# FFN of a routed expert layer turned round: weights stationary, 320 token lanes per expert moving, rows scattered to expert regions instead of gathered by tile

## The reference

```python
x = x + attention(layernorm(x), ctx_1024, ctx_1024, Wq, bq, Wk, bk, Wv, bv)
xt = layernorm(x)                                  # 1024 tokens x 128
scores = xt @ gate_w.T                             # 8 experts
top_vals, top_idx = top_k(scores, 2); top_w = softmax(top_vals)
h  = silu(xt @ w1[e].T) * (xt @ w3[e].T)           # hidden 512, for each expert e
ye = h @ w2[e].T
x  = x + sum over the two chosen experts of top_w * ye
```

## Time and profile before

| | us |
|---|---|
| median of the runs | 136.7 |
| span of the profiled execution | 132.1 |
| PE busy in it | 102.9 |
| POOL busy | 84.8 |
| DVE busy | 78.5 |
| ACT busy | 44.1 |
| span from the first up product (L974) to the last w2 product (L1007) | 46.9 to 120.7 |

### The profile page before, as it was taken

The page is one execution under the profiler, slowest core; times in us unless marked ns, Lnnn a source line. Parts: engine busy times, 40 slices in busy tenths (PEclk is TensorE's granted clock), DMA queues, the critical chain, the costliest instruction groups (busy, mean ns, idle before and its releaser), DMA issues. The chain is left out here.

```text
span 132.1 us, 2609 instructions
## 1 busy us (share of the span) xinstructions
PE 102.9 (78%) x571; PEld 71.5 (54%) x571; DVE 78.5 (59%) x276; ACT 44.1 (33%) x109; POOL 84.8 (64%) x122
## 2 busy tenths in 40 slices
PE   6869976789899279998977897997897979993000
PEld 2245962525355057886866675765675756762000
DVE  0862589897897969996745554563465545632000
ACT  4035877647700013343242033333234033331000
POOL 3387008383975926498769968969979697573630
PEclk9999999869599955999999999999999999999855
DMA  3969999500130002032232322202222323222220
GB/s 108 264 250 424 424 429 404 171 6 0 48 113 18 23 9 39 0 45 24 36 45 40 40 32 27 40 20 40 40 40 40 36 24 40 36 24 20 20 20 0
DMA packets 8119, 11.42 MB, mean 86 GB/s; under 512 B 880, under 2 KB 6896, under 8 KB 7344
## 3 DMA queue, kind: packets, MB, share of 16 engines
q1 hardware_dynamic: 4592, 8.70, 17.7%
q0 software_dynamic: 3520, 2.64, 15.6%
HBM read 8.91 MB, written 2.43 MB: 86 GB/s over the span
## 5 line engine op out<-in xcount | busy, mean ns | idle before, releaser
L381 POOL DMA_INDIRECT out_rows<-y_sb,aid x20 | 31.9, 1595 | 13.9 <-SPq L290 6.4
L523 ACT ACTIVATE hidT<-bank 128x256 f32<-128x256 f32 x40 | 13.5, 382 | 45.6 <-PE bank L997 37.6
L1007 PEld LDWEIGHTS bank<-w_sb,hidT 128*128 128x128 f32 x160 | 19.6, 191 | 7.6 <-issue 7.0
L1007 PE MATMUL bank<-w_sb,hidT 128*128 x160 | 22.4, 283 | 1.6 <-ACT hidT L523 0.9
L360 POOL DMA_INDIRECT xg<-tok_rows,gid x18 | 18.4, 1020 | 7.5 <-DVE slot_w L764 3.4
L974 PE MATMUL bank<-w_hi,xgT 128*128 x40 | 20.1, 503 | 3.0 <-DVE xgT L756 3.0
L910 PE MATMUL bank<-ones 128*128 128x512 bf16 x66 | 20.5, 463 | 1.1 <-DVE ones L544 1.1
L516 ACT ACTIVATE sil<-bank 128x512 f32<-128x512 f32 x20 | 12.1, 603 | 13.9 <-PE bank L976 12.1
L773 DVE TENSOR_TENSOR hid<-bank,sil 128x512 f32<-128x512 f32 x20 | 13.8, 690 | 4.6 <-PE bank L976 2.6
L975 PE MATMUL bank<-w_lo,xgT 128*128 x40 | 16.5, 413 | 0.0
L976 PE MATMUL bank<-w_hi,xgT 128*128 x40 | 16.5, 412 | 0.0
(11 more groups left out here) (120 smaller groups left out, 144.3 us busy)
## 6 DMA issues: line engine op xcount, KB each, us to landing
w_sb<-in_w1T SPq DMA_DIRECT2D x2, 1024.0 KB, 9.9
w_sb<-in_w3T SPq DMA_DIRECT2D x2, 1024.0 KB, 13.6
w_sb<-in_w2T SPq DMA_DIRECT2D x2, 1024.0 KB, 17.2
tok_rows<-tok SPq DMA_DIRECT2D x1, 520.0 KB, 4.4
x_sb<-in_x SPq DMA_DIRECT2D x2, 256.0 KB, 3.2
out_rows<-x SPq DMA_DIRECT2D x2, 256.0 KB, 4.7
ctxT_sb<-in_ctxT SPq DMA_DIRECT2D x1, 480.0 KB, 5.1
out_rows<-y_sb,aid POOLq DMA_INDIRECT x20
```

What stands on the lines that cost most here:

```text
L381: nc.gpsimd.indirect_dma_start(out[:, :], bass.IndirectOffsetOnAxis(ap=aid[p][:, 0:1], axis=0), y_sb[p][:, :], None, compute_op=ALU.add).t ...
L523: nc.scalar.activation(hidT[p][:, h * H // 2:(h + 1) * H // 2], ps_hT[h][:, 0:H // 2], ACT.Copy).then_inc(s_hidT, 1)
L1007: last = mm(ps_y[:, 0:D], hidT[p][:, c * P:(c + 1) * P], w2_sb[:, bass.ds(e * H + c * D, D)], start=(c == 0), stop=(c == HC - 1))
```

## The change

The FFN is written anew, and with it what feeds it.

- Routing: each expert owns `REG` rows of a DRAM table `expert_rows`, the first `CAP` = 320 of them for its normal lanes. `count_before` adds the start of the region (one more small matmul with `region`), so that DVE gets the row of each choice with one product and one reduction (`slots`). One-hot products, tiles, `gather_id`, `add_id` and expert words are gone.
- SP first fills the normal lanes of all regions with empty rows (16 DMAs of 520-byte rows, 1.33 MB, between w3 and w2 in its queue). Then POOL writes each token's row to the regions of both its experts: 16 indirect DMAs of 128 rows, `s_put`. When all have landed, SP reads the regions back (two DMAs for each expert).
- FFN: eight experts, each with 320 moving lanes. PE transposes three blocks of rows, runs four times (w1 chunk, w3 chunk) and four w2 products, all plain 32-bit with 128 x 128 weights stationary, and transposes the result back in three blocks. ACT does SiLU and the copies, DVE the product and the weighing, POOL three indirect adds for each expert, after the adds of the expert before have landed.
- Tokens past 320 of one expert would go through a loop of overflow steps; DVE works out its tables (`overflow_table`, 17 more linked instructions) ahead of the FFN. With the counts above the loop runs zero times.
- No high and low parts of weights or tokens. ACT copies the normalised rows once more (`twin_rows`). The normalisation of group 1 is moved ahead of `top_two(0)`.

```diff
+CAP = 320
+LANES = [min(P, CAP - at) for at in range(0, CAP, P)]
+KT = len(LANES)
@@ sync @@
+            weights(w1_sb, w1T, s_w1)
+            weights(w3_sb, w3T, s_w3)
+            sp.wait_ge(s_empty, 2)
+            for e in range(E):
+                for rows, lanes, k in pieces(e):
+                    sp.dma_start(rows, empty_rows[0:lanes, k, :]).then_inc(s_filled, 16)
+            weights(w2_sb, w2T, s_w2)
...
-            sp.dma_start(rows, tok[:, :, :]).then_inc(s_rows, 16)
+            for t in range(B):
+                sp.wait_ge(s_put[t], 16 * K2)
+            for e in range(E):
+                for rows, lanes, k in pieces(e):
+                    sp.dma_start(xg[0:lanes, e, k, :], rows).then_inc(s_xg[e], 16)
@@ gpsimd @@
+            pool.wait_ge(s_filled, 32 * E)
+            for g in range(G):
+                pool.wait_ge(s_slot, g + 1)
+                pool.wait_ge(s_pw, 3 * (g + 1))
+                pool.wait_ge(s_twin, g + 1)
+                for t in range(g * TG, (g + 1) * TG):
+                    for c in range(K2):
+                        nc.gpsimd.indirect_dma_start(
+                            expert_rows[:, :], bass.IndirectOffsetOnAxis(ap=slot[:, c, t:t + 1], axis=0),
+                            tok[:, c, t, :], None).then_inc(s_put[t], 16)
...
+            for e in range(E):
+                if e:
+                    pool.wait_ge(s_add, 16 * KT * e)
+                if e == OV_AT:
+                    overflow()
+                for k in range(KT):
+                    pool.wait_ge(s_ysb, KT * e + k + 1)
+                    m = LANES[k]
+                    nc.gpsimd.indirect_dma_start(
+                        out[:, :], bass.IndirectOffsetOnAxis(ap=xg[0:m, e, k, D:D + 1].bitcast(U32), axis=0),
+                        y_sb[e % 2][0:m, k, :], None, compute_op=ALU.add).then_inc(s_add, 16)
@@ scalar @@
-            high_parts(0, 6)
             copy_x2nT(0)
-            high_parts(6, 11)
+            twin_rows(0)
             copy_x2nT(1)
...
@@ vector @@
-            normalise(1, 0, x1, x2n, s_x2n)
+            normalise(1, 0, x1, tok[:, 0], s_x2n)
             norm_stats(1, 1, x1)
+            normalise(1, 1, x1, tok[:, 0], s_x2n)
             dve.wait_ge(s_const, 11)
             top_two(0)
-            normalise(1, 1, x1, x2n, s_x2n)
+            pair_weights(0)
+            slots(0)
             top_two(1)
...
+            def hidden(j):
+                dve.wait_ge(s_sil, j + 1)
+                dve.wait_ge(s_b, j + 1)
+                if j >= HC:
+                    dve.wait_ge(s_d, j - HC + 1)
+                dve_.tensor_tensor(hT[j % HC][:, :], ps_b[j % 2][:, 0:CAP], sil[j % 2][:, :],
+                                   ALU.mult).then_inc(s_hid, 1)
+            def weigh(e):
+                dve.wait_ge(s_yr, e + 1)
+                if e > 1:
+                    dve.wait_ge(s_add, 16 * KT * (e - 1))
+                for k, m in enumerate(LANES):
+                    dve_.tensor_scalar(y_sb[e % 2][0:m, k, :], ps_yr[0:m, k * D:(k + 1) * D],
+                                       xg[0:m, e, k, D + 1:D + 2], None, ALU.mult).then_inc(s_ysb, 1)
@@ tensor @@
+            for t in range(B):
+                pe.wait_ge(s_put[t], 16 * K2)
+                keep_busy(ps_av, 5)
...
+            turn_rows(0)
+            for j in range(E * HC):
+                e, c = j // HC, j % HC
+                if j == HC * (OV_AT + 1):
+                    overflow()
+                up(j)
+                if j > 1:
+                    down(j - 2)
+                if c == 2 and e + 1 < E:
+                    turn_rows(e + 1)
+                if c == 3 and e:
+                    turn_out(e - 1)
+            down(E * HC - 2)
+            down(E * HC - 1)
+            turn_out(E - 1)
```

More of the change, by code:

```diff
@@ L163, in build @@
[L163 to L167, removed]
+        slot = sb("slot", [P, K2, B], U32)
+        count = sb("count", [P, E])
+        ov_over = sb("ov_over", [P, E, OVT])
+        ov_n = sb("ov_n", [P, E])
+        ov_end = sb("ov_end", [P, E])
+        ov_total = sb("ov_total", [P, 1], I32)
@@ new lines, in overflow @@
+            def overflow():
+                with pool.Fori(0, n) as i:
+                    pool.wait_ge(s_ovy, i + 1)
+                    pool.sem_inc(s_ovgo, 1)
+                    nc.gpsimd.indirect_dma_start(
+                        out[:, :], bass.IndirectOffsetOnAxis(ap=ov_id[:, 0:1], axis=0), ov_y, None,
+                        compute_op=ALU.add).then_inc(s_ovadd, 16)
+                    pool.wait_ge(s_ovadd, 16 * i + 16)
+                    pool.sem_inc(s_ovid, 1)
+            n = overflow_steps(pool)
@@ L530, in _, with overflow @@
[L530 to L538 removed]
+            n = overflow_steps(act)
+            def overflow():
+                with act.Fori(0, n) as i:
+                    act.wait_ge(s_ovt, i + 1)
+                    nc.scalar.activation(ov_xT, ps_ovxT, ACT.Copy).then_inc(s_ovxT, 1)
+                    act.wait_ge(s_ova, i + 1)
+                    nc.scalar.activation(ov_sil, ps_ova, ACT.Silu).then_inc(s_ovsil, 1)
@@ new lines, in copy_yT @@
+            def copy_yT(e):
+                act.wait_ge(s_d, HC * (e + 1))
+                if e > 1:
+                    act.wait_ge(s_yr, e - 1)
+                nc.scalar.activation(yT[e % 2][:, :], ps_y[e % 2][:, 0:CAP], ACT.Copy).then_inc(s_yT, 1)
+            copy_xgT(0)
+            for e in range(E):
+                if e == OV_AT + 1:
+                    overflow()
+                for c in range(HC):
+                    silu(HC * e + c)
+                    if c == 1 and e:
+                        copy_yT(e - 1)
+                    if c == 2 and e + 1 < E:
+                        copy_xgT(e + 1)
@@ L816, in _ @@
+            overflow_table()
+            for e in range(E):
+                if e == OV_AT + 1:
+                    overflow()
+                for c in range(HC):
+                    hidden(HC * e + c)
+                if e:
+                    weigh(e - 1)
+            weigh(E - 1)
         @block.tensor
@@ L913, in _ @@
             pe.wait_ge(s_ones, 1)
-            keep_busy(ps_rank[1], 14)
+            for i in range(8):
+                keep_busy(bank[i], 2)
             pe.wait_ge(s_const, 3)
```

736 lines of the change are left out of this document (250 added, 486 removed).

## The result

| | before | after |
|---|---|---|
| median of the runs, us | 136.5 (4 runs, 135.67 to 137.67) | 142.91 (4 runs, 140.83 to 143.42) |
| ratio, 95% interval | | 1.045 (1.032 to 1.059) |
| span of the profiled execution, us | 132.1 | 141.3 |
| that execution's own time, us | not known | 143.06 |
| PE busy, us | 102.9 | 104.9 |

What follows compares the result with a forecast made beforehand. PE's pace bounds the loop, POOL close behind. Front + 9.7, loop - 14.5, slow start - 1.1, tail + 6.3 sum to + 0.4 on the 132.1 span; with 4.6 outside it 137.1 us, range 129.5 to 146.

Steps and rivals of the forecast that it cites:

- The overflow loop: Loop of overflow steps in the FFN: taken to run zero times, given no term in the sum and no rival.
- PE's pace: FFN loop: 0.54 us a product, 0.59 for the transposes in and out, 7.05 us an expert, 56.4 for eight.
- The clock: Start of the FFN: PE's clock falls to half after a 2.9 us pause, 2.3 us lost, bounds 0 and 2.8.
- The front: Up to the first up product: first scatter at 30.0, 1.32 us a step, first up product at 56.6, 9.7 later.
- The fills: Front: filling the regions with empty rows ends at 26 expected, 30 at full price, hardly in the way.
- The tail: After the last w2 product: adds wait for landings, 7.1 us a group; 17.7 us instead of 11.4, + 6.3.
- The median above the span: Outside the span: 4.6 us added to the 132.5 span, as the median before stood that far above its span.
- Scatter at the price of an add: Slower rival, front: a scatter costs what an add does, 8.7 us later, 146.2; chance 0.3 together with the DVE stop.
- POOL stopped by DVE: Slower rival, front: DVE's work holds up POOL's scatters, ending 7.2 us later, 144.3; chance 0.3 together with the dearer scatter.
- No gaps and a full clock: Faster rival: scatters and adds without 0.30 us gaps, clock holds at the FFN's start, 129.1 us; chance 0.3.
- the slower side of the forecast: Whole kernel: a time above the 134.0 to 139.4 us counted as same; chance 0.34.

Runs made afterwards that it cites:

- e1: The changed kernel with the five overflow loops left out, their tables kept: 137.52 us, ratio to before 1.011.
- g1: The changed kernel with each overflow loop kept inside a condition that skips it at zero steps: 136.86 us, runs too scattered for a ratio.
- e2: e1 with 10 useless PE products behind each landed token tile instead of 5, 12 behind the last: 135.61 us, ratio to before 0.999.
- c4: Changed kernel, overflow loops behind a condition, results turned one chunk earlier, 5 useless products behind tiles 0 to 3, 10 behind 4 to 7: 132.79 us, ratio 0.978.
- c5: c4 with 10 useless products only behind token tiles 6 and 7, 5 behind all others: 132.90 us, ratio to before 0.979.
- s1: e1 with only each token's first choice scattered, 8 indirect DMAs instead of 16: 126.34 us, ratio to before 0.932.
- e3: e1 with the 16 fills issued ahead of w1 instead of behind w3: 137.36 us, ratio to before 1.004.
- t1: e1 with the three adds of expert 6 left out, all products kept: 131.39 us, ratio to before 0.960.
- e4: e2 with each expert's result turned and weighed one chunk earlier in the next expert: 134.73 us, too wide for a ratio.

## Why the prediction missed by 5.8 us, point by point

Of the span, 132.5 was forecast and 141.3 came: 8.8 us more. The allowance for what lies outside it was 4.6 and came as 1.8: 2.8 less. The median lies 0.15 below the profiled execution. Together 5.8. The terms of the span below sum to 8.7 of the 8.8.

- **The overflow loop, + 5.1.** This is the step that failed, and it failed in the reading of the code. The forecast took its cost at nothing, from the sentence that the loop runs zero times. The trace of before has no such loop and could not confirm that. So it was an unknown to be bounded, with a rival of its own, and none stood there. e1 and g1 show it.
- **PE's pace, + 2.4.** The product was sized right, 0.54 (from 0.404 for 480 columns by columns). The turns were not: 0.59 forecast for in and out, from four transposes in a row. The steps of PE after are 0.51 from the first row transpose to the up product, 0.10 more until the next (0.64 instead of 0.54), and 0.33 for the turn out. That is 0.94, and 7.41 us an expert instead of 7.05. The forecast named this miss as the likeliest small one ("7.3 instead of 7.05 alone is + 2").
- **The clock, + 0.5.** Six products took 6.17 us (57.02 to 63.19) and would take 3.33: 2.8 lost, where 2.3 was taken and 2.8 was the upper bound. That the clock would be half at the start of the FFN was right, and e2 shows what it costs by holding it. The reason given was not: the forecast had the clock fall in PE's pause of 2.9 us behind the last products with no use. It had fallen before them, between 52 and 53, and c4 keeps it through the same pause. The size came out all the same, which is luck.
- **The front, + 0.4.** Row numbers at 30.14 (29.9 forecast), fills landed at 30.55 (26 expected, "at most 30" said), step 1.265 (1.32), last scatter landed 2.3 us after its start (2.75), read back 2.9 with both issues (2.9), S at 57.02 (56.6). The first scatter started 1.07 us late, of which the row numbers have 0.24; most of the rest is the 0.9 us between row numbers and first scatter, for which the forecast had 0.1. The cheaper scatter (15 steps, 0.6) and its earlier landing (0.4) cancel this, and what is left, 0.4, is the transposes at half clock. The fills cost nothing here, as forecast, but about 1 us in e1, c5 and s1. The forecast had them landed at 26 or 30; the median landing was 7.5 to 7.9 us behind each issue, the last at 30.55.
- **The tail, + 0.3.** The turn of expert 6 to its first add took 1.7 instead of 1.0, for it waited for the landing of the group before. Then group 6.94 (7.1), last add + 3.74 (3.8), end + 6.9 (7.1).
- **The median above the span, - 2.8.** I added 4.6 us because the median of before stood that far above the profiled span. In the runs since, time less span was 1.7 to 2.4 us for nearly every execution of any kernel, of before too (136.88 with a span of 135.0). So the profiled execution of before was a short one, and the earlier trace rows come from a run of about 134 us. The right working was before's usual span, 134.5, against 132.5: a gain of 2 us, which the terms for pace, clock, front and tail (3.6) turn into a loss of 1.6 for the kernel without the loop pass; e1 measured a loss of 1.5. That before's profiled execution was a short one is argued from these numbers, since its own time is not known.

The rivals. Scatter at the price of an add: no, 0.96 against 1.56 in the same trace, and the size of the step was the forecast's. POOL stopped by DVE: no. The Trainium skill (SBUF — State Buffer, "Who interferes with whom") was weighed for it. DVE was busy 2.59 of the 3 us from 36 to 39 and 0 from 45 to 48, and the scatters take 0.95 to 0.98 us in both; no run here shows a stop. The rule is about the two-port modes alone; whether DVE was in one there, no view tells, so the forecast's "each scatter would wait out" took more from it than it says. The longer 1.23 of the first one is there in every kernel and belongs to the first of a series, as in the earlier trace rows, where I had put 0.27 us down to DVE. No gaps and a full clock (129.1): the gaps of 0.30 stayed, the clock fell, and c4 shows that the clock could be had.

So the slower side of the forecast had its chance from two mechanisms that don't show here, and the one that made the kernel slower had none. That 142.9 lies inside the wide range is luck.

## What to carry to other kernels

Ask of every loop with a count from data what it does at a count of zero: read it in the trace, and put a condition ahead of it, which cost nothing here and saved 5 us. A stage that goes through DRAM with one indirect DMA per 128 rows is paid on POOL at a fixed step (16 x 1.26 us, nearly all of it on the path), so count such DMAs before counting the products that the new order saves. Filler work that holds a clock must be sized for the slower clock, since it may be there that it runs first: half the filler in the early batches, and ten in place of twelve in the last, were worth 2.7 us. And the wait that a view names last isn't yet the price of what was waited for: it takes a kernel in which that wait is gone, as e3 for the fills.

## What the hardware showed that I had not expected

- An indirect DMA costs POOL by the instruction, little by the row: an add of 128 rows 1.56 us, of 64 rows 1.43; a plain scatter of 128 rows 0.96; the first of a series 1.23. Between two in a row with no wait there are 0.30 us in every kernel here.
- PE's clock stayed full from 43 to 52 us with 5.05 of 9 us busy, and fell in the same pattern between 52 and 53 in the changed kernel and before 50 in t1 and c5. Before, it had come back at 39 (e4) to 43 us (g1), in kernels that differ little up to there. What decides it can't be read from these rows.
- A landing to DRAM behind POOL's instruction takes 2.3 us for a scatter and 2.8 to 3.2 for an add. The Trainium skill (DMA: Bandwidth & Descriptors, "Anatomy of one DMA — SWDGE (gpsimd) path") gives about 2 us as fixed cost, most of it the receipt of the write; the scatter's landing here is of that size, the add's up to half as much again. The row count moves it little: 2.84 us behind the issue of a 64-row add in e1, 3.17 behind one of 128 rows.
